# Four fp32 tiles of the first routed experts computed ahead of the other 35, and a new table of leads for what comes after

## The reference, cut to what matters

```python
t = _rmsnorm(x, g2).reshape(-1, D)                       # 2048 tokens, D = 256
probs = jax.nn.softmax(t @ router_w, axis=-1)            # E = 8 experts
vals, idx = jax.lax.top_k(probs, K)                      # K = 2
w = vals / jnp.sum(vals, axis=-1, keepdims=True)
gate = jnp.sum(jax.nn.one_hot(idx, E, dtype=t.dtype) * w[..., None], axis=1)
hid = jax.nn.silu(jnp.einsum('td,edf->tef', t, w1)) * jnp.einsum('td,edf->tef', t, w3)   # F = 512
y_e = jnp.einsum('tef,efd->ted', hid, w2)
y = jnp.einsum('ted,te->td', y_e, gate)
return res + y.reshape(b, s, D)
```

## Time and profile before

| | |
|---|---|
| device time, median of 3 runs | 916.08 us (915.75 to 916.25) |
| device time of the profiled execution | 916.48 us |
| its span, first to last instruction | 914.6 us |
| busy in the span | PE 854.8, DVE 709.8, ACT 607.7, POOL 278.1 us |
| mean granted TensorE clock | 0.992 of full speed |

### The profile page before, as it was taken

One profiled execution on the slowest core, in us unless ns is written; L12 is line 12 of the kernel. 1 busy time (PEld: TensorE's weight loads), 2 busy tenths in 40 slices (PEclk: granted clock), 3 DMA queues, 4 the chain that ended last, 5 costly groups with the idle time before them and its releaser, 6 DMA issues.

```text
span 914.6 us, 23436 instructions
## 1 busy us (share of the span) xinstructions
PE 854.8 (93%) x7788; PEld 766.7 (84%) x7788; DVE 709.8 (78%) x1976; ACT 607.7 (66%) x1719; POOL 278.1 (30%) x359
## 2 busy tenths in 40 slices
...
GB/s 313 80 131 257 310 24 25 31 88 93 53 59 59 151 48 48 52 24 133 35 25 25 59 83 47 82 60 25 24 169 167 389 92 89 103 97 96 105 118 195
DMA packets 43032, 92.92 MB, mean 102 GB/s; under 512 B 6081, under 2 KB 29505, under 8 KB 41505
## 3 DMA queue, kind: packets, MB, share of 16 engines
...
HBM read 62.22 MB, written 29.17 MB: 100 GB/s over the span
## 4 chain that ended last, share of the span: by engine, by line
PE 65%; DVE 8%; issue 2%; DMA 2%; ACT 1%; POOL 1%; ACTq 0%; DVEq 0%; POOLq 0%
PE ps L982 17%; PE ps L788 11%; PE ps L789 11%; PE ps L790 11%; PE ps L1075 3%; PE ps L1099 3%; PE ps L1085 3%; PE ps L1157 2%; DMA BIG<-ys_dram,YI 2%; DVE BIGR L1903 1%; PE ps L954 1%; PE ps L955 1%; DVE X L1938 1%; PE ps L944 1%; ACT BIGR L1304 0%
## 5 line engine op out<-in xcount | busy, mean ns | idle before, releaser
L788 PE MATMUL ps<-BIGR 128*128 128x256 f32 (+1 forms) x970 | 298.4, 308 | 9.0 <-DVE BIGR L1903 3.9
L790 PE MATMUL ps<-BIGR 128*128 128x256 f32 (+1 forms) x922 | 262.7, 285 | 0.0
L789 PE MATMUL ps<-BIGR 128*128 128x256 f32 (+1 forms) x746 | 218.6, 293 | 0.0
L788 PEld LDWEIGHTS ps<-BIGR 128*128 128x128 f32 x970 | 185.4, 191 | 18.4 <-issue 14.2
L982 PE MATMUL ps<-BIG 128*128 128x128 f32 x1424 | 180.5, 275 | 0.0
L790 PEld LDWEIGHTS ps<-BIGR 128*128 128x128 f32 x922 | 175.9, 191 | 0.7
L982 PEld LDWEIGHTS ps<-BIG 128*128 128x128 f32 x1424 | 169.9, 192 | 0.1
L789 PEld LDWEIGHTS ps<-BIGR 128*128 128x128 f32 x746 | 143.3, 192 | 1.9
...
L1443 ACT ACTIVATE BIG<-ps,BIG 128x128 f32<-128x128 f32 x256 | 91.4, 384 | 15.4 <-DVE BIG L1983 15.2
L2132 POOL DMA_INDIRECT xs_dram<-TT,PI x64 | 65.9, 1030 | 73.1 <-ACT PI L1284 58.4
L2154 POOL DMA_INDIRECT yt_dram<-BIG,IX x47 | 45.8, 974 | 124.0 <-DVE BIG L1896 121.2
(10 more groups left out here) (264 smaller groups left out, 1857.2 us busy)
## 6 DMA issues: line engine op xcount, KB each, us to landing
...
BIG<-xs_dram SPq DMA_DIRECT2D x39, 128.0 KB, 2.0
ys_dram<-BIG SPq DMA_DIRECT2D x39, 128.0 KB, 1.7
...
```

The costliest lines, as they stand in the source:

```text
L788: pe.matmul(o, l[0], r[0], start=start, stop=False)
L789: pe.matmul(o, l[0], r[1], start=False, stop=False)
L790: return pe.matmul(o, l[1], r[0], start=False, stop=stop)
```

## The change

Four of the tiles (`AHEAD`) are taken out of the list and are computed earlier, by a path of their own. When ten blocks (`COUNTED`) have been counted, `a_route` on DVE lists four full tiles from the rows that these blocks have scattered; the main list then begins behind them. `NT0` falls from 39 to 35, `PAIRED` from 18 to 14 and 21 single tiles remain. For an early tile i, SP loads the rows (`a_xs`), PE reads the expert's number into a register (`a_reg`) and transposes (`a_xT`); ACT scales (`a_xT_e`); PE computes `a_gate` and `a_up` in plain fp32 with the weights as they lie, as two matmuls of 512 columns each (`a_gate0`, `a_gate1`, `a_up0`, `a_up1`); ACT and DVE do `a_silu` and `a_hm`; PE transposes the hidden rows (`a_hT`, four transposes), ACT copies them (`a_hT_e`), PE runs four matmuls of 256 columns (`a_down0`, `a_down1`), ACT copies the result (`a_y`) and SP stores it (`a_ys`). No weight is split for these tiles. Their buffers are blocks of the context that the latent attention has read, so SP loads 10 of the 16 blocks again later (`ct_back`), and `ch` of the cross attention waits for that. The filling matmuls of the passage go (`FILL` 30 to 0). `places` gets a part for the rows of early tiles. The leads of the latent attention stay, those of later phases are new.

```diff
-NT0 = 32 + E0 - 1
+AHEAD = 4
+COUNTED = 10
+AHEAD_DUE = 400
+assert 128 * (AHEAD - 1) < 2 * COUNTED * 128 - E0 * 127
+NT0 = 32 + E0 - 1 - AHEAD
 NT1 = 32 + E1 - 1
 
-PAIRED = 2 * -(-(2 * NB * 128 - E0 * 255) // 256)
+PAIRED = 2 * -(-(2 * NB * 128 - 128 * AHEAD - E0 * 255) // 256)
-FILL = (30, 24)
+FILL = (0, 24)
+AHEAD_ROWS = (8, 9, 10, 11, 6, 7)[:AHEAD]
...
-    800, "cnt": -200, "cpow": 900, "ctxh": -500, "down1": -5000, "epow": -3300, "eps3": -7000, "exp0": 100, "exp1":
...
+    "ys0": -36015, "ys1": -20787
...
+    ahead_phases(p)
     p.add("DVE", 4800, ("route", 0), ("rb", 0, NB - 1))
...
+def ahead_phases(p):
+    p.add("DVE", 2200, ("a_route",), ("rb", 0, COUNTED - 1), due=AHEAD_DUE)
+    for i in range(AHEAD):
+        def add(engine, ns, name, *after, banks=(), **kw):
+            p.add(engine, ns, (name, i), *after, banks=[("s", (q, i)) for q in banks], due=AHEAD_DUE + 20 * i, **kw)
+        add("SP", 700, "a_xs", ("a_route",), ("sc", 0, COUNTED - 1), ("ctx", COUNTED - 1), ("load_w0b",), late=2200)
+        add("PE", 600, "a_reg", ("a_route",), ("load_w0b",))
+        add("PE", 220, "a_xT", ("a_xs", i), ("s", NB - 1), banks=["a_xT_e"])
+        add("ACT", 310, "a_xT_e", ("a_xT", i), ("a_up1", i - 2))
+        add("PE", 860, "a_gate0", ("a_xT_e", i), ("a_reg", i), banks=["a_silu"])
+        add("PE", 860, "a_gate1", ("a_gate0", i))
+        add("PE", 860, "a_up0", ("a_gate1", i), banks=["a_hm"])
+        add("PE", 860, "a_up1", ("a_up0", i))
+        add("ACT", 470, "a_silu", ("a_gate1", i), ("a_hT", i - 2))
+        add("DVE", 600, "a_hm", ("a_up1", i), ("a_silu", i))
+        add("PE", 450, "a_hT", ("a_hm", i), banks=["a_hT_e"])
+        add("ACT", 490, "a_hT_e", ("a_hT", i), ("a_down1", i - 2), *[("ctx", b) for b in (13,) if i % 2])
+        add("PE", 860, "a_down0", ("a_hT_e", i), banks=["a_y"])
+        add("PE", 860, "a_down1", ("a_down0", i))
+        add("ACT", 330, "a_y", ("a_down1", i))
+        add("SP", 60, "a_ys", ("a_y", i), late=2000)
+    p.add("SP", 100, ("ct_back",), ("a_ys", AHEAD - 1), ("down", 0, 4), late=8000)
...
-    p.add("SP", 100, ("load_kv",), ("down", 0, PAIRED - 1), due=0, late=12000)
+    p.add("SP", 100, ("load_kv",), ("down", 0, PAIRED - 1), ("a_down1", AHEAD - 1), due=0, late=12000)
...
-            add("ACT", 520, ("ch", j), *over, ("V", ctx_before(j), 1, 1), ("K", ctx_before(j), 1, 1))
+            add("ACT", 520, ("ch", j), ("ct_back",), *over, ("V", ctx_before(j), 1, 1), ("K", ctx_before(j), 1, 1))
...
-            add("POOL", 2550, ("ga", 0, b), ("ys", 0, NT0 - 1), ("places",), ("pro1", b - 2),
+            add("POOL", 2550, ("ga", 0, b), ("ys", 0, NT0 - 1), ("a_ys", AHEAD - 1), ("places",), ("pro1", b - 2),
...
-        YS = nc.dram_tensor("ys_dram", [NT0 * 128, D], F32, kind="Internal").ap()
+        YS = nc.dram_tensor("ys_dram", [(NT0 + AHEAD) * 128, D], F32, kind="Internal").ap()
...
+        ct_ = CT[:, :, :, :].rearrange("p b k t -> p (b k t)")
+        AXS = [ct_[:, b * D:b * D + D] for b in AHEAD_ROWS]
+        AXT = [btg[:, :], small1[:, 0:D]]
+        AH = [ct_[:, b * D:b * D + F0] for b in (2, 4)]
+        AHT = [ct_[:, b * D:b * D + F0] for b in (0, 12)]
+        behind, ahead_row = AE[:, 0:E0], AE[:, E0:2 * E0]
...
+            def a_reg(i):
+                if i == 0:
+                    pe.wait_ge(sem("ahead_listed"), 1)
+                    pe.wait_ge(sem("wgu_loaded"), 32)
+                    pe.wait_ge(sem("wd_loaded"), 16)
+                expert[i] = pe.value_load(AI[i:i + 1, 0:1], min_val=0, max_val=E0 - 1)
+
+            def a_xT(i):
+                vacant(pe, "a_xT", i)
+                pe.wait_ge(sem(f"rows_loaded{i % 3}"), 16 * (i // 3 + 1))
+                pe.transpose(ps("a_xT", i)[:, 0:128], AXS[i][:, 0:128], ident)
+                pe.transpose(ps("a_xT", i)[:, 128:256], AXS[i][:, 128:256], ident).then_inc(*fills("a_xT", i))
+
+            def a_gate_up(i, which, k):
+                key = f"a_{which}0", i
+                if k == 0:
+                    vacant(pe, *key)
+                    if which == "gate":
+                        pe.wait_ge(*emptied("a_xT", i))
+                at = k * 2 * F0 + (F0 if which == "up" else 0)
+                m = pe.matmul(ps(*key)[:, :], AXT[i % 2][:, k * 128:k * 128 + 128],
+                              WGU[:, bass.ds(expert[i] * (4 * F0) + at, F0)], start=k == 0, stop=k == 1)
+                if k == 1:
+                    m.then_inc(*fills(*key))
+
+            def a_hT(i):
+                vacant(pe, "a_hT", i)
+                pe.wait_ge(*emptied("a_up0", i))
+                for c in range(4):
+                    at = slice(c * 128, c * 128 + 128)
+                    m = pe.transpose(ps("a_hT", i)[:, at], AH[i % 2][:, at], ident)
+                m.then_inc(*fills("a_hT", i))
+
+            def a_down(i, x):
+                key = "a_down0", i
+                if x == 0:
+                    vacant(pe, *key)
+                    pe.wait_ge(*emptied("a_hT", i))
+                for c in (2 * x, 2 * x + 1):
+                    m = pe.matmul(ps(*key)[:, 0:D], AHT[i % 2][:, c * 128:c * 128 + 128],
+                                  WD[:, bass.ds(expert[i] * (2 * F0) + c * D, D)], start=c == 0, stop=c == 3)
+                if x == 1:
+                    m.then_inc(*fills(*key))
...
+                    act.wait_ge(sem("tiles_listed"), r + 1)
...
+            def a_xT_e(i):
+                act.wait_ge(*full("a_xT", i))
+                if i >= 2:
+                    act.wait_ge(*full("a_up0", i - 2))
+                for k in range(2):
+                    at = slice(k * 128, k * 128 + 128)
+                    m = act.mul(AXT[i % 2][:, at], ps("a_xT", i)[:, at], g2c[:, k:k + 1])
+                    if k:
+                        m.then_inc(*frees("a_xT", i))
+
+            def a_silu(i):
+                act.wait_ge(*full("a_gate0", i))
+                if i >= 2:
+                    act.wait_ge(*full("a_hT", i - 2))
+                act.activation(AH[i % 2], ps("a_gate0", i)[:, :], ACT.Silu).then_inc(*frees("a_gate0", i))
+
+            def a_hT_e(i):
+                act.wait_ge(*full("a_hT", i))
+                if i >= 2:
+                    act.wait_ge(*full("a_down0", i - 2))
+                if i == 1:
+                    act.wait_ge(*full("ctx", 13))
+                act.copy(AHT[i % 2], ps("a_hT", i)[:, :]).then_inc(*frees("a_hT", i))
+
+            def a_y(i):
+                act.wait_ge(*full("a_down0", i))
+                act.copy(AXS[i], ps("a_down0", i)[:, 0:D]).then_inc(*frees("a_down0", i))
+
             def ch(jj):
+                if jj < 2:
+                    act.wait_ge(sem("ct_loaded2"), 16 * len(EARLY_KV) + 32)
...
+            def a_route():
+
+                E, steps = E0, [RP[:, 32 * i:32 * i + 16] for i in range(4)]
+                nn, te, rr, w1 = sc_[:, 0:E], sc_[:, 32:33], sc_[:, 34:35], RC[:, 224:224 + E]
+                tiles = OHW[0].rearrange("p a n -> p (a n)")[:, 0:E * AHEAD].rearrange("p (n j) -> p n j", n=E)
+                v.tensor_tensor(nn, CNT[:, COUNTED, 0:E], ecap[0], ALU.subtract).then_inc(dv, next_step("dve"))
...
+                v.scalar_tensor_tensor(out=w1, in0=iota[0][:, 0:E], scalar=te, in1=ahead_row, op0=ALU.is_equal,
+                                       op1=ALU.mult).then_inc(dv, next_step("dve"))
+                v.tensor_copy(AI[:, 0:1], te).then_inc(dv, next_step("dve"))
+                then()
+                v.tensor_reduce(rr, w1, AX, ALU.add).then_inc(dv, next_step("dve"))
+                then()
+                v.tensor_scalar(AI[:, 1:2], rr, cst["j128"], None, ALU.add).then_inc(sem("ahead_listed"), 1)
+                v.tensor_scalar(ahead_row, ahead_row, -128.0 * NT0, None, ALU.add).then_inc(dv, next_step("dve"))
+
+            def a_hm(i):
+                v.wait_ge(*full("a_up0", i))
+                v.wait_ge(*emptied("a_gate0", i))
+                v.tensor_tensor(AH[i % 2], ps("a_up0", i)[:, :], AH[i % 2], ALU.mult).then_inc(*frees("a_up0", i))
...
+                then()
+                for i, t in enumerate((ahead_row, behind)):
+                    v.tensor_tensor(OHw, oh, t.rearrange("p (o n) -> p o n", o=1).broadcast_to([128, 2 * NB, E]),
+                                    ALU.mult).then_inc(dv, next_step("dve"))
+                    then()
+                    v.tensor_reduce(RP[:, 32 * i:32 * i + 32], OHw, AX, ALU.add).then_inc(dv, next_step("dve"))
+                    then()
+                v.tensor_tensor(RP[:, 0:32], pf, RP[:, 0:32], ALU.subtract).then_inc(dv, next_step("dve"))
+                v.tensor_tensor(RP[:, 32:64], pf, RP[:, 32:64], ALU.is_lt).then_inc(dv, next_step("dve"))
+                then()
+                v.tensor_tensor(RP[:, 0:32], RP[:, 0:32], Y1[:, :], ALU.subtract).then_inc(dv, next_step("dve"))
+                then()
+                v.tensor_tensor(RP[:, 0:32], RP[:, 0:32], RP[:, 32:64], ALU.mult).then_inc(dv, next_step("dve"))
+                then()
```

(41 more changed lines are left out.)

52 lines of the change are left out of this document (36 added, 16 removed), and 25 rows, old and new, of the table LEAD.

## The result

The changed kernel takes 928.65 us (median; 928.29 to 929.62), the kernel before 916.16 over four runs, the three of the table above and one of 918.74. The ratio on record is 1.0118, 95% interval 1.0091 to 1.0146. The medians differ by 12.5 us, and a ratio of 1.0118 makes 10.8 of 916.16: slower either way, where 911 had been forecast.

A forecast was written before the change was run, and what follows sets the result against it. PE was taken as the bound, busy 854.8 of 914.6 us. The terms -18.0 + 4.3 + 4.1 + 2.0 + 2.3 = -5.3 us, from the median 916.08, gave 911 us, range 904.5 to 916.5.

The forecast's parts named there:

- The rest: Small DMAs, context reload, and new leads in the cross attention and behind it: 0 us, bounds -3 and +2.
- the 18.33 of 20 for the pairs: Paired tiles: DVE busy 18.33 of 20 us, close behind PE; DVE becoming the bound there was a rival, chance 0.14.
- Four paired tiles go, four early ones come: Experts: four paired tiles fewer save 18.0 us; early-tile work left among the main tiles adds 4.3 us.
- effective start of 211.7: First `gate` before the change: began at 209.24 us, counted as 211.7 in full-speed terms because the clock was low.
- 512 columns at 0.86 us: Early tiles: one fp32 matmul of 512 columns was taken to cost 0.86 us, from 0.84 to 0.90.
- The passage, +4.1: Between latent attention and first experts: first `gate` at 215.8 us against 211.7, costing 4.1 us (1.9 to 6.4).
- The wait of 1.1 us that was forecast at `a_hT` 0: Passage: PE would wait about 1.1 us because `a_hm` 0 stands behind `route` and `gates_b` on DVE.
- the rival of the clock: Passage: early tiles run at 1.2 GHz, making the kernel slower, 921 to 927.5 us; chance 0.10.
- the row of 184 to 186 us: Before the change: PE busy 1.46 of 2 us, clock 1.00; taken to show the clock stays up despite waits.
- `places`, +2.0: Paired tiles: longer `places` on DVE makes PE wait up to 3.0 us instead of 0.6; +2.0 us taken.
- A clock of 0.50 behind 200 us: Sign of being wrong: a granted clock of 0.50 behind 200 us.
- Where the experts end, +2.3: Last `down` waits 2.6 us for split weights, first `Q` up to 0.8: +2.3 us (1.5 to 3.0).

The follow-up runs named there:

- E4: Changed kernel with the last experts' pair of row operations back behind the weight copy and the last result store ahead of the query loads: 914.77 us, 0.9970 of before.
- E1: Changed kernel with the last experts' pair of short row operations put back behind the weight copy of the tile before: 920.78 us, ratio 1.0035.
- E5: Changed kernel, same order on every engine, but VectorE reads the expert number of tile j+2 right behind the hidden product of tile j: 920.35 us, ratio 1.0033.
- E3: Kernel before, with only the last experts' pair of row operations moved right ahead of its tile's weight copy, no early tiles: 927.73 us, ratio 1.0113.
- E2: Changed kernel with the last result store of the first experts moved back ahead of the two query weight loads: 924.83 us, ratio 1.0081.
- E6: E4 with the K projections between the last two down phases and the last tile's VectorE work ahead of the second weights': 914.41 us, ratio 0.9962.
- E7: E6 with `places` cut in two, the part added for early tiles standing behind the last paired `hl`: 912.59 us, ratio 0.9946.

## Why the prediction was wrong

**The step that failed is "The rest", put at 0 with bounds of -3 and +2.** It took up the transfers that the early tiles add and the waits of PE behind 400 us, and called the new leads an exchange of neighbours. Two of these exchanges cost most of the 17.6 us that lie between 911 and 928.65: with both undone (E4) the ratio falls from 1.0118 to 0.9970, by 13.6 us. E1 puts the number's read at 7.6 us (a ratio of 1.0035 against 1.0118), E5 at 7.8, E3 at 10; E2 and E4 put the store at 3.4 to 6.0. Neither was in a rival: the one case that ended slower was about the clock.

The read could not be found by looking at PE's waits before, for there were none in the last experts. VectorE was close to being the bound there, with 0.20 us idle ahead of the copy in a period of 2.72. Its timeline of that loop, read as the prediction read the 18.33 of 20 for the pairs, would have said that what is put into VectorE's loop counts 46 times.

**The other steps, in order.**

- *Four paired tiles go, four early ones come*: right as far as the stage tells. From the effective start of 211.7 to the first single tile the stage took 80.5 us before and 70.4 from 217.54 here: 10.1 less, where -18.0 + 4.3 + 2.0 = -11.7 had been forecast; `places` took more than the difference (below).
- *512 columns at 0.86 us*: right, 0.85.
- *The passage, +4.1*: +5.8. `wup` slipped by 2.3 us, not 1.1, and the clock, low since 184.5, is part of it. The wait of 1.1 us that was forecast at `a_hT` 0 did not come: PE reached it at 207.71, behind the end of `a_hm`. A wait of 1.40 came where none was forecast, at `a_up0` 0 (202.09): it writes the same PSUM bank as `a_gate0` 0, so `a_silu` 0 must empty the bank first, and on ACT a table load of 1.28 us stood ahead of `a_silu`. That the sizes are alike is luck. From 200 us to the first `gate` the clock was 1.00, so the rival of the clock fell for the early tiles. The terms here are no finer than some 3 us: in the traces of the seven versions with this passage the first `gate` lies between 216.7 (E5) and 219.9 (E6), and the clock fell and rose at other moments in each. The argument that the row of 184 to 186 us shows the clock staying up did not hold even for the changed kernel's trace (0.62 there). Two readings of the working were off: of the 14.64 busy us from 200 to 220 some 2.5 are the fill, which ends at 202.53, not 7.5; and a mean of 0.90 over 214 to 216 puts the rise at 214.4, not 214.2, which moves 211.7 by 0.1. The windows of the passage (columns as in the earlier trace rows):

```profile
196.00:198.00 2.00, 2.00 (x4) 0.68 (x3) 0.62 (x5) 0.28 (x2) 1.23 (x2) 0.50 0.15 51
198.00:200.00 2.00, 2.00 (x10) 1.10 (x9) 1.36 (x9) 0.57 (x2) 1.52 (x3) 0.97 0.11 41
200.00:202.00 2.00, 0.69 (x2) 0.00 (x0) 1.82 (x11) 1.97 (x5) 0.69 (x1) 1.00 0.26 90
...
212.00:220.00 8.00, 8.00 (x38) 5.19 (x38) 5.29 (x10) 4.71 (x11) 0.00 (x0) 1.00 0.39 119
280.00:300.00 20.00, 16.69 (x131) 16.57 (x131) 12.03 (x19) 8.33 (x14) 0.00 (x0) 0.91 0.51 174
```

- *`places`, +2.0*: the mechanism was right and the size low. The wait is 3.3 us against 0.60 in the earlier trace rows, +2.7. Behind it the clock was at its lower level until 287: the matmuls came every 0.21 us where they come every 0.12 at the higher level, 15 of them, which cost some 1.5 us more. The sum had no term for the clock behind a wait. A clock of 0.50 behind 200 us was among the signs of being wrong; it came, but not in the early tiles.
- *Where the experts end, +2.3*: the wait at the last `down` came, somewhat longer than forecast (3.27 for 2.6 us), and the first `Q` waited 0.57 us longer, inside the 0.8 that was allowed for it. E6 took 1.3 us of the wait away, of which 0.8 came back at the `NT` phases; by the ratios it brought 0.7 us (0.9970 to 0.9962), inside the noise. What the whole wait costs is not shown.

With the two exchanges undone (E4) the kernel is 0.3% faster than before, 2.7 us, where the sum gave 5.3. E7 reaches 5 us, but that does not confirm the sum: it takes away part of two waits that the sum had already charged with 2.0 and 2.3.

What stays open: 2.3 us by which the last experts' tiles still take longer in E1 than before from first `gate` to last (127.4 against 125.1). In the changed list `SD 4 0` stands behind the first `gate` of that stretch instead of ahead of it; two such phases took 3.62 us in the earlier trace rows, so one phase of 1.8 us has moved into the stretch, which by itself costs the kernel nothing and would explain 1.8 of the 2.3. No run tried it.
